# Weighted sums of a row in two stretches, and latent keys behind the selected scores

## The reference, cut to what matters

```
a1 = _attn(q, k1, v1, causal=True)     # latent keys
a2 = _attn(q, ks, vs, causal=False)    # 32 selected tokens
a3 = _attn(q, kw, vw, causal=True)     # window keys
out = g[:, 0] * a1 + g[:, 1] * a2 + g[:, 2] * a3
...
_attn: softmax(q @ k.T * scale, masked) @ v
```

## Time and profile before

| | |
|---|---|
| runs | 1951.96, 1947.19, 1948.29 us |
| profiled execution | 1946.69 us, of which the trace's span is 1944.9 us |
| share of the span busy | PE 92%, VectorE 61%, ScalarE 63%, GpSimd 35% |
| mean granted TensorE clock | 0.963 of 2.4 GHz |

### The profile page before, as it was taken

One profiled execution on the slowest core, in us unless ns is written; L12 is line 12 of the kernel. 1 busy time (PEld: TensorE's weight loads), 2 busy tenths in 40 slices (PEclk: granted clock), 3 DMA queues, 4 the chain that ended last, 5 costly groups with the idle time before them and its releaser, 6 DMA issues.

```text
span 1944.9 us, 33816 instructions
## 1 busy us (share of the span) xinstructions
PE 1789.4 (92%) x10588; PEld 1034.9 (53%) x10588; DVE 1180.4 (61%) x3695; ACT 1228.5 (63%) x3383; POOL 688.9 (35%) x697
## 2 busy tenths in 40 slices
PE   5666689999999999999999999999999999999998
PEld 3333445555556545655555555555565555555554
DVE  5999565556556555655655555555555565555565
ACT  3564366766666656666676666665666667667664
POOL 0565533433333233333334333332333333433300
PEclk8787699999999999999999999999999999999999
DMA  4001111112111211211111211121121111121101
GB/s 163 1 1 27 26 50 39 39 41 59 26 40 37 50 34 39 50 43 50 39 39 35 59 26 39 36 46 44 39 50 43 50 39 39 37 59 26 40 22 44
DMA packets 71295, 80.91 MB, mean 42 GB/s; under 512 B 29520, under 2 KB 37840, under 8 KB 70992
## 3 DMA queue, kind: packets, MB, share of 16 engines
q1 hardware_dynamic: 71120, 78.76, 16.4%
HBM read 7.91 MB, written 2.10 MB: 5 GB/s over the span
## 4 chain that ended last, share of the span: by engine, by line
PE 57%; DVE 16%; issue 12%; POOL 7%; ACT 3%; SPq 3%; DMA 1%; DVEq 0%; POOLq 0%; ACTq 0%
PE bank L1862 19%; PE bank L1883 12%; PE bank L1825 8%; PE bank L1716 3%; PE bank L1715 2%; SPq L541 2%; DVE arena L1451 2%; PE bank L1779 2%; PE bank L1836 2%; PE bank L1773 1%; DVE arena L1228 1%; PE bank L1788 1%; PE bank L1711 1%; PE bank L1782 1%; POOL arena L698 1%
## 5 line engine op out<-in xcount | busy, mean ns | idle before, releaser
L1451 DVE CUSTOM_DVE_ANT_0 arena<-bank,W 128x512 f32<-128x512 f32 (+3 forms) x1024 | 478.4, 487 | 557.8 <-PE bank L1862 544.1
L999 ACT ACTIVATE arena<-arena 128x512 f32<-128x512 f32 (+3 forms) x1024 | 569.0, 556 | 333.1 <-DVE arena L1451 329.1
L1862 PE MATMUL bank<-arena 96*128 96x512 f32 (+3 forms) x2048 | 700.6, 444 | 0.0
L1862 PEld LDWEIGHTS bank<-arena 96*128 96x128 f32 x2048 | 351.8, 192 | 192.5 <-issue 148.5
L1883 PE MATMUL bank<-W,arena 128*128 128x128 f32 x2560 | 430.7, 282 | 9.6 <-ACT arena L999 7.3
L1883 PEld LDWEIGHTS bank<-W,arena 128*128 128x128 f32 x2560 | 296.7, 142 | 239.3 <-issue 168.2
L991 ACT ACTIVATE arena<-bank 128x512 f32<-128x512 f32 (+1 forms) x512 | 277.6, 542 | 177.2 <-PE bank L1883 173.3
L736 POOL TENSOR_TENSOR arena<-arena,one 128x512 f32<-128x512 f32 x64 | 66.6, 1041 | 777.4 <-DVE arena L1419 606.5
L1825 PE MATMUL bank<-arena 128*32 128x256 f32 (+1 forms) x3072 | 222.8, 362 | 18.6 <-DVE arena L1462 17.1
L999 ACT ACTIVATION_READ_ACCUMULATOR arena<-arena 128x1 f32 x1024 | 194.8, 190 | 0.0
L1825 PEld LDWEIGHTS bank<-arena 128*32 128x32 f32 x3072 | 61.8, 108 | 206.0 <-issue 150.3
(11 more groups left out here) (257 smaller groups left out, 2086.3 us busy)
## 6 DMA issues: line engine op xcount, KB each, us to landing
arena<-arena SPq DMA_DIRECT2D x896, 64.0 KB, 2.0
arena<-arena SPq DMA_DIRECT2D x64, 128.0 KB, 2.3
W<-wide SPq DMA_DIRECT2D x1, 3730.0 KB, 13.3
X<-x SPq DMA_DIRECT2D x8, 256.0 KB, 5.8
out<-arena SPq DMA_DIRECT2D x8, 256.0 KB, 2.3
arena<-arena SPq DMA_DIRECT2D x96, 16.0 KB, 1.8
LW<-lat SPq DMA_DIRECT2D x1, 768.5 KB, 14.3
arena<-mods SPq DMA_DIRECT2D x1, 768.0 KB, 4.6
```

What stands on the lines that cost most here:

```text
L999: done = A(here, here, ACT.Exp, bias=nmax[:, c:c + 1], scale=-1.0, accum_out=lsum[:, c:c + 1])
L1451: last = v.tensor_tensor_reduce(Pb[:, s % 4, at_p:at_p + n], bank[turn.score_bank(s)][:, at:at + n], w("mask", T - n), -1.0, 3e38, ALU.add ...
L1862: last = MM(B_[:, at:at + n], query(t), Kb[a][g % 2][0:QD, h, 0:n], start=True, stop=True)
```

## The change

All pieces of the tall tiles of a row are issued together in step 12 from the row's start, and both pieces of the low tiles in step 15, after `spread` where both are due. `values` loses its argument c and loops over it. In group 0, the scores of the selected keys (`s2`) move from step 10 to 9 and the latent keys of the next group (`nk1`) from step 9 to 11; in the first group of all, `s2` from 10 to 9 and `nk1` from 9 to 10.

```
-PV_TALL, PV_LOW = 10, 14
+PV_TALL, PV_LOW = 12, 15
...
     if g == 0:
-        steps, proj = {"op": 7, "s2": 10, "o2": 20}, (0, 1, 3, 6, 8, 5, 9, 21, 22)
+        steps, proj = {"op": 7, "s2": 9, "o2": 20}, (0, 1, 3, 6, 8, 5, 11, 21, 22)
...
     if first:
-        proj = (0, 1, 3, 6, 8, 5, 9, 14, 16)
+        proj = (0, 1, 3, 6, 8, 5, 10, 14, 16)
...
-                def values(r, low, c):
+                def values(r, low):
...
-                    if c == 0:
-                        if low == 0:
+                    if low == 0:
                         ... (waits: row before normed, values read, PT moved)
                     top = 1 if low else 3
-                    n = P if c == top else 2 * P
-                    for h in range(HG):
-                        ... MM(bank[5][rows, ...], V[...][:, c, rows], PT[low][:, h, ...])
-                    if c == top:
-                        last.then_inc(s_pv, 1)
+                    for c in range(top + 1):
+                        n = P if c == top else 2 * P
+                        for h in range(HG):
+                            ... the same MM
+                    last.then_inc(s_pv, 1)
...
-                    for low, at, parts in ((0, PV_TALL, 4), (1, PV_LOW, 2)):
-                        r, c, known = turn.rows(s, at)
-                        if known and c < parts:
-                            values(r, low, c)
                     r, late, known = turn.rows(s, SPREAD)
                     if known and late == 0:
                         spread(r)
+                    for low, at in ((0, PV_TALL), (1, PV_LOW)):
+                        r, late, known = turn.rows(s, at)
+                        if known and late == 0:
+                            values(r, low)
```

More of the change, by code:

```diff
@@ L1805, in attend @@
                 n_units, u0, p0 = len(turn.units), turn.u0, turn.p0
-                def values(r, low, c):
+                def values(r, low):
                     q, a = divmod(r, GR)
-                    if c == 0:
-                        if low == 0:
[L1811 to L1820, removed]
-                    top = 1 if low else 3
-                    n = P if c == top else 2 * P
-                    for h in range(HG):
-                        rows = slice(h * VH, (h + 1) * VH)
-                        last = MM(bank[5][rows, low * 2 * P:low * 2 * P + n], V[a][turn.g(q) % 2][:, c, rows],
-                                  PT[low][:, h, c * 2 * P:c * 2 * P + n], start=(c == 0), stop=(c == top))
-                    if c == top:
-                        last.then_inc(s_pv, 1)
@@ new lines, in values @@
+                    if low == 0:
+                        done = turn.r0 + r
+                        if not (isinstance(done, int) and done == 0):
+                            pe.wait_ge(s_nrm, done)
+                        else:
+                            pe.wait_ge(s_scr, 1)
+                        if a == 0:
+                            pe.wait_ge(s_ga, turn.read("vl", q) if ("vl", q) in turn.index else turn.act0)
+                    last_unit = r * RU + (RU - 1 if low else 2 * HG - 1)
@@ new lines, in values @@
+                    pe.wait_ge(s_pd, turn.moved(last_unit, "dve"))
+                    pe.wait_ge(s_pa, turn.moved(last_unit, "act"))
+                    top = 1 if low else 3
+                    for c in range(top + 1):
+                        n = P if c == top else 2 * P
+                        for h in range(HG):
+                            rows = slice(h * VH, (h + 1) * VH)
+                            last = MM(bank[5][rows, low * 2 * P:low * 2 * P + n], V[a][turn.g(q) % 2][:, c, rows],
+                                      PT[low][:, h, c * 2 * P:c * 2 * P + n], start=(c == 0), stop=(c == top))
```

## The result

The changed kernel takes 1862.76 us, the median of four runs (1861.88 to 1863.67), against 1947.74 (1944.48 to 1951.96) before: a ratio of 0.9563, 95% interval 0.9543 to 0.9582. The forecast was 1852 us, the range 1838 to 1892. The gain is 85 us where 96 were worked out. The profiled executions differ by 83.3 us (1946.69 and 1863.37). Lines behind 1828 have moved up by one: what was 1862, 1883 and 1836 is 1861, 1882 and 1835.

The account below looks back on a forecast made before the run. Outside the prologue, only what TensorE's queue holds or waits for was taken to count. 72 + 6 + 17 + 5 - 3.5 = 96.5 us off the profiled 1946.69 gives 1850.2, as a median 1852 us; range 1838 to 1892.

Parts of the forecast that it names:

- The visit's price, 0.28 us: Each TensorE visit to the weighted sums costs 0.28 us whatever it computes; four fewer a row save 72 us.
- rival B: A visit's cost belongs to the piece, not the change of shape; merging saves only waits, 25 us, 1924; chance 0.06.
- The seams: At the four new seams of a row in the merged visits, weight loads cost nothing; at most 28 us.
- rival A: Every seam between merged rounds shows its weight load: 28 us less gain, 1880 us; chance 0.15.
- Tall sums later, low sums at 15: Tall sums at step 12 save 6 us of waiting for ScalarE; low sums at 15 save 17.1 us for VectorE.
- the cover of 0.4 us: In rows a = 1 TensorE reaches the low sums 0.4 us after VectorE's move 11 ends, so nothing waits.
- the 0.8 ahead of group 0's scores: Operands for group 0's first scores still land in time, with 0.8 us to spare after TensorE's way shortens.
- Rival C: Covers are thinner than thought, overrun by 1 us each in 24 rows and 7 batches: 31 us less, 1883; chance 0.10.
- Given back in step 11: The step 11 transposes wait 0.2 us in two of four groups of each batch: 3.5 us given back.
- `s2` and `nk1`: In group 0 the wait at `s2` passes to `z4T`, 2.6 us there; moving both tasks gains 5 us in all.
- group 0's low-sum wait (0.9 us a batch): Group 0's part of the 17.1 us of low-sum waits for VectorE, counted as gained in full.
- Rival D: The long tall visit starves VectorE and ScalarE: slower, 2001 us, or 1966 with rows a = 1 alone; chance 0.05.

Follow-up runs that it names:

- experiment 3: The changed kernel with the tall sums cut into two visits, in steps 12 and 13, same matmuls: 1885.96 us.
- experiments 1 and 2: Each part alone on the kernel before: the merged sums without moving `s2` and `nk1`, 1888.89 us; the moved tasks with the old sums, 1942.05 us.
- Experiment 9: The changed kernel with GpSimd's norm power first, then the copy for the spread (`repeat`), then the rotation of the keys: 1836.12 us.
- experiment 6: The changed kernel with tall and low sums in one visit a row, in step 14 ahead of `spread`: 1890.58 us.
- experiment 4: The changed kernel with GpSimd's norm power ahead of the key rotation in group 0, the copy still behind the rotation: 1857.12 us.

## Why the prediction was right, and where it was off

**The visit's price, 0.28 us (right).** Both visits came out within 0.02 us, and experiment 3 gives 0.28 for one visit more. So rival B (the cost belongs to the piece) is out. A visit also changes the bank and the operands, but so does each step from scores to transposes, and the earlier trace rows leave nothing over for that: the scores of a low step have two rounds of 256 columns and two of 128, the transposes 3 x 128, and at 0.22 us for 256 columns these are the 0.66 and 0.33 us that they take. What is left, by elimination, is the change to 32-column tiles. The Trainium skill, "TensorEngine Tiling (Array Packing)" (Key Properties), says that a change of tiling mode drains the array. That fits, though no view shows the drain itself.

**The seams (right).** Taken at nothing by the loads of the earlier trace rows, they cost nothing: 32 records in 1.72 us, as eight rounds of 0.22 or less leave no room for a load of 0.11 us. The last twelve loads lie between 965.21 and 965.77, under matmuls that run on without a break:

```profile
965.21 0.56 PEld L1825 LDWEIGHTS bank<-arena 128*32 128x32 f32 x12
```

The Trainium skill's rule that weight loads overlap only where the row group differs ("TensorE: Matmul & The Clock Gate", The mechanism) doesn't hold for these tiles, where the trace decides; rival A is out.

**Tall sums later, low sums at 15 (right).** The scores of steps 10 and 11 without a tall piece take 0.65 (0.76 behind a long fill), not 0.84. No row waits for line 1462 at the sums any more; the cover of 0.4 us held, and so did the 0.8 ahead of group 0's scores, where no DMA is waited for. Rival C is out.

**Given back in step 11 (half right).** In group 1 the transposes of step 11 come 0.85 us behind the scores, 0.65 in a plain step: the 0.2 is there, seven times. In group 3 it is 0.76, no more than a step behind a long fill takes anyhow, and group 3 gained 0.6 us a batch more than the sum says. The waits for line 999 in the table (7.1 us in 20 places) aren't these; they stand in steps of tall tiles, before (7.3 in 19) as after.

**`s2` and `nk1` (mechanism right, size off).** The wait went from `s2` to z4T as said: z4T starts 11.23 us after step 9 of group 0 (11.2 forecast), behind line 1350, seven times in the full batches, 2.42 us each. What the sum had at "5 us" is worth 5 alone and 26 behind the merge (experiments 1 and 2): the split into terms was wrong where the total was nearly right, for the merge's own terms were counted as if TensorE didn't run into the wait sooner. They make 72 + 6 + 17 - 3.5 = 91.5 us, and the merge alone brought 58. That the total came so near is in part luck: one term was 33 too large, the other 21 too small.

**The step that was mis-sized: group 0 behind the new wait.** The prediction expected the low clock behind the new wait too, but has no term for it, and took group 0's low-sum wait (0.9 us a batch) as gained on top. From step 9 of group 0 to z4T, and from z4T to the end of the group, one batch of before and one of the change (columns as above):

```profile
1102.87:1115.97 13.10, 10.45 (x61) 5.05 (x60) 6.72 (x31) 5.12 (x19) 8.17 (x8) 0.87 0.32 90
1115.97:1141.40 25.43, 24.43 (x147) 14.77 (x146) 14.91 (x50) 17.19 (x44) 2.96 (x5) 1.00 0.12 28
...
1457.50:1468.73 11.23, 8.62 (x69) 4.77 (x68) 5.82 (x30) 5.24 (x19) 8.19 (x8) 1.00 0.32 92
1468.73:1492.94 24.21, 23.91 (x122) 15.54 (x122) 14.52 (x46) 17.06 (x44) 2.96 (x5) 0.93 0.15 36
```

Before, the low clock lay ahead of z4T, in six batches of seven; now z4 alone fixes z4T's start, and the low clock lies behind it, where nothing covers it. By span and granted clock it costs 10.3 us in the seven groups 0 before and 11.9 now: hardly more, in another place. In the mean of the seven, the way to z4T is 1.6 us shorter, where the terms have about 0.9 (an estimate: 0.5 for `s2`, 0.35 for three visits made one, 0.09). The way behind it is 1.2 us shorter, where they have 3.2. It would be 2.6 at full clock, as the two batches without a low clock show (22.8 us); steps 14 and 22 are short of the rest.

In five of the seven batches the scores of step 14 run at half the clock (1.71 us for 0.86). The stretch of this step in one of them, columns as above:

```profile
1468.70:1470.34 1.64, 1.61 (x10) 1.32 (x10) 1.60 (x6) 1.11 (x3) 0.17 (x1) 0.89 0.40 94
1470.34:1473.60 3.26, 3.26 (x12) 2.07 (x12) 3.00 (x8) 1.59 (x4) 2.79 (x5) 0.53 0.44 103
```

The granted clock is 0.53 of 2.4 GHz, so nearly all of it at 1.2, between 1.6 and 4.9 us behind the end of the wait; TensorE was busy throughout and had been idle for 2.4 of the 3 us before. Step 14 was to shrink by 1.7 us (5.15 to 3.46, with a low piece and a wait less) and shrank by 0.18 in the median; at full clock it takes 3.74. With what the neighbouring steps gained, group 0 is 1.2 us a batch short: 8 us, the largest part of the 13 that are missing in the profiled executions (96.5 worked out, 83.3 found). Group 3 gives 4 back, and batches slower than the median take 4. Experiment 9 confirms it from the other side: with the wait gone, step 14 takes 3.59.

**The tail (not in the sum).** From the start of the last scores to TensorE's last instruction the kernel takes 35.3 us, 32.9 before: the last low sums stand behind a spread that waits 1.87 us for GpSimd's copy, and the first four matmuls behind them take 3.22 us, 1.98 before. Together that is 2.4 us.

```profile
1827.50 0.66 PE L1835 MATMUL bank<-W,arena 128*128 128x128 f32 x4 [1.87 <-POOL arena L736]
1828.09 1.27 PE L1825 MATMUL bank<-arena 128*32 128x256 f32 x16
1829.29 3.22 PE L1926 MATMUL bank<-arena,W 128*128 128x512 f32 x4
```

What is left, some 3 us in the first and the last batch, wasn't traced to a place.

**Rival D** had a real core that the runs showed only elsewhere: work moved on TensorE's queue does change what covers a wait. The tall visit in step 12 covers 1.65 us of GpSimd's chain; taken away, group 0 loses them (experiment 6).

## What to carry to other kernels

Sums that share a tile shape belong behind one another: each visit to the 32-column products cost 0.28 us beside what it computed, and the rounds joined without a seam. A wait that a merge uncovers grows by what the merge saves ahead of it, so terms of a sum around one wait have to be taken together, at the arrival of both sides. Where a short chain crosses GpSimd, look at what stands ahead of it in GpSimd's queue and at what runs beside VectorE's part of it: 27 us came here from three calls in another order, with no instruction less.

## What had not been expected of the hardware

- Four float32 TENSOR_SCALARs over 128x128 took 4.90 us beside GpSimd's TENSOR_TENSORs and 1.12 without them; the other way round, a TENSOR_TENSOR of GpSimd's took 1.54 us instead of 1.09 beside VectorE's two-operand work (experiment 9, 1055.00). Having the input 5.5 us sooner (experiment 4) brought 6 us, removing the overlap as well 21 more.
- The low clock and the wait that it followed are loosely tied. Behind the same wait of 2.42 us it came in five batches of seven. It began between 0.4 us ahead of the wait's end and 1.3 us behind it, and held at a granted 0.5 for 3.4 us in three of the five and for 6.8 in two. In the other two batches the steps ran at full clock; what decides between them stays open.
